# One-core attention and feed-forward block: causal mask for the row maxima added by VectorE instead of TensorE, layer norm spread over GpSimd and ScalarE, and a separate step order for each engine

## The reference

```python
xn = layernorm(x)                                    # over the last axis, eps 1e-5
q, k, v = xn @ Wq.T, xn @ Wk.T, xn @ Wv.T            # 16 heads of 16
att = q @ k.T / sqrt(16) + causal_mask               # per batch and head, 512 x 512
s = (softmax(att) @ v) @ Wo.T
gate, up = silu(qlinear(xn, wq_gate)), qlinear(xn, wq_up)   # 256 -> 704, integer weights less 128, times scale
g = silu(qlinear(gate * up, wq_down))                # 704 -> 256
out = x + s * g
```

## Time and profile before

| what | value |
|---|---|
| median of 3 runs | 343.9 us (339.8 to 346.67) |
| the profiled execution | 341.76 us |
| its span, first to last instruction | 340.0 us |
| mean granted TensorE clock | 0.975 |

### The profile page before, as it was taken

How to read it: one execution, slowest core, us unless ns; L and a number is a source line. 1 busy time by engine, 2 the same in 40 slices (tenths; PEclk the granted TensorE clock), 3 DMA queues, 4 the chain that set the end, 5 groups by cost and what they waited for, 6 DMA issues and landing times.

```text
span 340.0 us, 6041 instructions
## 1 busy us (share of the span) xinstructions
PE 304.1 (89%) x2352; PEld 207.2 (61%) x2352; DVE 215.4 (63%) x359; ACT 168.1 (49%) x239; POOL 133.2 (39%) x190
## 2 busy tenths in 40 slices
PE   0688688999999989999999999999999999998873
PEld 0566456787565547688665556688665656884433
DVE  5799787445569986646568986646465656455223
ACT  3527134634556655524456655524466666235830
POOL 4077344411254563202354463202355563123351
PEclk9999697999999999999999999999999999999996
DMA  7947671049670004078580010078590020010201
GB/s 281 255 155 174 188 119 63 4 155 151 191 128 1 2 3 126 13 201 155 178 143 2 2 64 2 7 191 144 188 157 4 0 67 4 0 35 31 66 0 64
DMA packets 21008, 31.56 MB, mean 93 GB/s; under 512 B 2148, under 2 KB 9956, under 8 KB 20980
## 3 DMA queue, kind: packets, MB, share of 16 engines
q1 hardware_dynamic: 20528, 30.50, 37.2%
q10 hardware_dynamic: 452, 0.67, 0.5%
HBM read 20.32 MB, written 10.49 MB: 91 GB/s over the span
## 4 chain that ended last, share of the span: by engine, by line
PE 70%; DVE 21%; ACT 3%; issue 2%; DMA 2%; POOL 0%; ACTq 0%; SPq 0%; DVEq 0%
PE ps L349 15%; PE ps L351 12%; PE ps L350 12%; PE ps L519 10%; PE ps L500 7%; PE ps L459 6%; PE ps L471 4%; DVE mx L958 2%; DVE mx L960 2%; DVE hid L945 2%; DVE nw L919 2%; DVE xn L926 2%; PE ps L527 2%; ACT hid L654 2%; DVE nw L920 1%
## 5 line engine op out<-in xcount | busy, mean ns | idle before, releaser
L859 POOL TENSOR_SCALAR_AFFINE_SELECT pt<-pt 128x256 f32<-128x256 f32 (+1 forms) x112 | 48.1, 443 | 117.3 <-ACT pt L719 117.3
L719 ACT ACTIVATE pt<-ps 128x1024 f32<-128x1024 f32 x80 | 81.8, 1023 | 23.6 <-PE ps L500 23.5
L827 POOL TENSOR_TENSOR hl<-hid,hh 128x512 fp32r<-128x512 f32 x24 | 31.2, 1300 | 42.7 <-ACT hh L668 42.3
L958 DVE TENSOR_REDUCE mx<-ps 128x2 f32<-128x1024 f32 x32 | 39.0, 1221 | 12.8 <-PE ps L471 12.4
L459 PE MATMUL ps<-kp,qp 48*128 48x512 f32 (+3 forms) x256 | 37.2, 350 | 10.9 <-DVE mx L958 6.9
L519 PE MATMUL ps<-pt,vt 128*17 128x256 f32 (+3 forms) x512 | 43.8, 437 | 1.2 <-POOL pt L859 1.1
L349 PE MATMUL ps<-xh,guh 128*128 128x512 f32 x96 | 43.2, 450 | 1.5 <-DVE u L939 1.5
L500 PE MATMUL ps<-qp,kp 50*128 50x512 f32 (+3 forms) x256 | 40.4, 373 | 2.5 <-DMA qp<-ctr 2.2
L821 POOL TENSOR_TENSOR hid<-hid 128x512 f32<-128x512 f32 x24 | 32.2, 1342 | 21.5 <-ACT hid L661 21.3
L351 PE MATMUL ps<-xh,gul 128*128 128x512 f32 x96 | 38.5, 401 | 0.0
L350 PE MATMUL ps<-xl,guh 128*128 128x512 f32 x96 | 38.3, 399 | 0.0
(11 more groups left out here) (107 smaller groups left out, 538.9 us busy)
## 6 DMA issues: line engine op xcount, KB each, us to landing
qk_scratch<-hid SPq DMA_DIRECT2D x24, 256.0 KB
qp<-qk_scratch SPq DMA_DIRECT2D x14, 256.0 KB, 4.7
kp<-qk_scratch SPq DMA_DIRECT2D x14, 256.0 KB, 6.8
qp<-qk_scratch SPq DMA_DIRECT2D x18, 128.0 KB, 5.1
kp<-qk_scratch SPq DMA_DIRECT2D x18, 128.0 KB, 7.2
xr<-in_x SPq DMA_DIRECT2D x4, 512.0 KB, 3.8
out<-xr SPq DMA_DIRECT2D x8, 256.0 KB, 2.2
xin<-in_x SPq DMA_DIRECT2D x3, 512.0 KB, 3.9
```

Source lines behind the costliest of these rows:

```text
L719: nc.scalar.activation(pt[:, 2 * kk:2 * kk + 2, :], ps[:, base:base + 2, :], ACT.Exp, scale=SCALE).then_inc(exp_done, 1)
L859: mm = nc.gpsimd.affine_select(out=diag, in_=diag, compare_op=ALU.is_ge, fill=0.0, base=0, pattern=[[0, diag.shape[1]], [1, P]], channel_m ...
L958: mm = nc.vector.tensor_reduce(mg[:, :, kk, 3], both, AX.X, ALU.max, negate=True)
```

## The change

- From the ninth pair on (`n >= LEAD`), TensorE's 4 mask matmuls of a pair are left out. VectorE adds a float32 triangle `tri` (128 x 128, broadcast) to the diagonal blocks in PSUM, in place, and waits for its own addition (`tri_added`) before it reduces. Pairs 0 to 7 of batch 0 keep the matmuls.
- The inverse root for batches 1 to 3 goes to GpSimd (`root`): 2 operations, three times 4, and 2 more that make `shf` = -mean * root, 16 in all, each waiting for the one in front. The first guess is made in one operation instead of two.
- The normalisation of batches 1 to 3 goes to ScalarE (`Identity` with scale and bias). VectorE keeps the statistics and their aggregation (`moments`).
- `hsg` and `sgt` are made by GpSimd.
- `FILL` is replaced by four tables, one for each engine, with 20 steps each. TensorE does the units first, then the scores, then the maxima.
- SP stores all four chunks of q and k first, then `c_rows(b, 2)`, then the first half of `stack`; the second half comes after `c_rows(b, 3)`.

```diff
+TENSOR_STEPS = (
+    [("pv", -1, 10), ("pv", -1, 11), ("s", 0, 0), ("m", 0, 8)],
+    [("zt", -1, 3), ("v", 0, 0), ("s", 0, 1), ("m", 0, 9)],
+    [("v", 0, 1), ("s", 0, 2), ("m", 0, 10)],
+    [("t", 1, 0), ("t", 1, 1), ("z2", -1, 1), ("pv", 0, 0), ("s", 0, 3), ("m", 0, 11)],
+    [("c", 0, 1), ("qk", 1, 0), ("qk", 1, 1), ("s", 0, 4), ("m", 0, 12)],
+    [("dn", 0, 0), ("s", 0, 5), ("m", 0, 13)],
+    [("qk", 1, 2), ("pv", 0, 1), ("s", 0, 6), ("m", 0, 14)],
+    [("dn", 0, 1), ("s", 0, 7), ("m", 0, 15)],
+    [("qk", 1, 3), ("o", -1, 0), ("pv", 0, 2), ("s", 0, 8), ("m", 0, 16)],
+    [("gu", 1, 0), ("c", 0, 2), ("pv", 0, 3), ("s", 0, 9), ("m", 0, 17)],
+    [("zt", 0, 0), ("gu", 1, 1), ("pv", 0, 4), ("s", 0, 10), ("m", 0, 18)],
+    [("o", -1, 1), ("gu", 1, 2), ("pv", 0, 5), ("s", 0, 11), ("m", 0, 19)],
+    [("gu", 1, 3), ("gu", 1, 4), ("s", 0, 12), ("m", 1, 0)],
+    [("gu", 1, 5), ("zt", 0, 1), ("s", 0, 13), ("m", 1, 1)],
+    [("c", 0, 3), ("gu", 1, 6), ("s", 0, 14), ("m", 1, 2)],
+    [("pv", 0, 6), ("gu", 1, 7), ("s", 0, 15), ("m", 1, 3)],
+    [("z2", 0, 0), ("gu", 1, 8), ("s", 0, 16), ("m", 1, 4)],
+    [("gu", 1, 9), ("pv", 0, 7), ("s", 0, 17), ("m", 1, 5)],
+    [("pv", 0, 8), ("c", 1, 0), ("gu", 1, 10), ("s", 0, 18), ("m", 1, 6)],
+    [("zt", 0, 2), ("gu", 1, 11), ("s", 0, 19), ("m", 1, 7), ("pv", 0, 9)],
+)
...
+VECTOR_STEPS = (
+    [],
+    [("max", 0, 8)],
...
+    [("max", 1, 1), ("norm", 0, 1)],
+    [("max", 1, 2), ("gate", 1, 3)],
+    [("max", 1, 3), ("zlo", 0, 0)],
+    [("max", 1, 4), ("gate", 1, 4)],
+    [("max", 1, 5)],
+    [("max", 1, 6), ("gate", 1, 5), ("norm", 0, 2), ("max", 1, 7)],
+)
...
@@ tensor: maxima
-                for r in range(2):
+                for r in range(2 if n < LEAD else 0):
...
@@ vector: maxima
+                if STEPS * b + m >= LEAD:
+                    if kk < 2:
+                        diag = both[:, :, 3 * P:]
+                        mask = tri[:].rearrange("p (o n) -> p o n", o=1).to_broadcast([P, 2, P])
+                    else:
+                        diag = (both[:, :, 2 * P:].rearrange("p e (a n) -> p e a n", a=2) if kk < 4 else
+                                both.rearrange("p e (a c n) -> p e a c n", a=2, c=2)[:, :, :, 1, :])
+                        mask = tri[:].rearrange("p (o q n) -> p o q n", o=1, q=1).to_broadcast([P, 2, 2, P])
+                    if STEPS * b + m == LEAD:
+                        dve.wait_ge(consts, 3)
+                    nc.vector.tensor_tensor(diag, diag, mask, ALU.add).then_inc(tri_added, 1)
+                    dve.wait_ge(tri_added, STEPS * b + m - LEAD + 1)
...
@@ gpsimd
+            def root(b, n):
+                v, y, t = nw[:, 0, :], nw[:, 1, :], nw[:, 2, :]
+                if n == 0:
+                    pool.wait_ge(mv_done, TT * b)
+                    pool.wait_ge(xn_done, TT * b)
+                    root_op(nc.gpsimd.tensor_scalar(v, mv[:, :, 1], EPS, None, ALU.add))
+                    root_op(nc.gpsimd.tensor_scalar(y.bitcast(I32), v.bitcast(I32), -0.5, MAGIC, ALU.mult, ALU.add))
+                    return
+                root_op(nc.gpsimd.tensor_tensor(t, y, y, ALU.mult))
+                root_op(nc.gpsimd.tensor_tensor(t, t, v, ALU.mult))
+                root_op(nc.gpsimd.tensor_scalar(t, t, -0.5, 1.5, ALU.mult, ALU.add))
+                root_op(nc.gpsimd.tensor_tensor(y, y, t, ALU.mult))
+                if n == NEWTON:
+                    root_op(nc.gpsimd.tensor_tensor(t, mv[:, :, 0], y, ALU.mult))
+                    nc.gpsimd.tensor_scalar(shf[:], t, -1.0, None, ALU.mult).then_inc(shf_done, 1)
...
@@ scalar
+            def normalise(b, i):
+                if i == 0:
+                    act_e.wait_ge(shf_done, b)
+                    act_e.wait_ge(xt_ready, KD * b)
+                nc.scalar.activation(xn[:, i, :], xin[:, i, :], ACT.Identity, scale=nw[:, 1, i:i + 1],
+                                     bias=shf[:, i:i + 1]).then_inc(xn_done, 1)
...
@@ sync
                 if b + 1 < B:
-                    store_qk(b + 1, 0)
-                    store_qk(b + 1, 1)
+                    for c in range(4):
+                        store_qk(b + 1, c)
+                c_rows(b, 2)
+                if b + 1 < B:
                     stack(b + 1, 0, 0)
                     stack(b + 1, 0, 1)
-                    store_qk(b + 1, 2)
-                    store_qk(b + 1, 3)
-                c_rows(b, 2)
                 if b:
                     store_out(b - 1, 0)
                     store_out(b - 1, 1)
+                c_rows(b, 3)
                 if b + 1 < B:
                     stack(b + 1, 1, 0)
                     stack(b + 1, 1, 1)
-                c_rows(b, 3)
```

More of the change, by code:

```diff
@@ new lines @@
+GPSIMD_STEPS = (
+    [("hlo", 0, 4), ("hid", 0, 5)],
+    [],
+    [("hlo", 0, 5), ("mask", 0, 0)],
+    [("mask", 0, 1)],
+    [("mask", 0, 2)],
+    [("mask", 0, 3)],
+    [("mask", 0, 4)],
+    [("mask", 0, 5)],
+    [("mask", 0, 6)],
+    [("mask", 0, 7)],
+    [("mask", 0, 8)],
+    [("res", -1, 0), ("hid", 1, 0), ("mask", 0, 9)],
+    [("hlo", 1, 0), ("mask", 0, 10)],
+    [("root", 2, 0), ("res", -1, 1), ("hid", 1, 1), ("mask", 0, 11)],
+    [("root", 2, 1), ("hlo", 1, 1), ("hid", 1, 2), ("mask", 0, 12)],
+    [("root", 2, 2), ("mask", 0, 13)],
+    [("root", 2, 3), ("hlo", 1, 2), ("mask", 0, 14), ("hid", 1, 3)],
+    [("mask", 0, 15)],
+    [("hlo", 1, 3), ("hid", 1, 4), ("mask", 0, 16)],
+    [("mask", 0, 17), ("mask", 0, 18), ("mask", 0, 19)],
+)
@@ L72, with entries @@
 HEAD_MIX = HEAD[6:]
[L75 to L84, removed]
+HEAD_DONE = {(k, 0, n) for k in ("t", "qk", "gu", "xhi", "xlo", "qhi", "qlo", "tanh", "up", "hhi", "gate", "hid", "hlo")
+             for n in range(2 * HT)}
+HEAD_DONE |= {("c", 0, 0), ("ccp", 0, 0)} | {(k, b, i) for k in ("bn", "mom", "root", "xn") for b in range(2) for i in range(TT)}
+def entries(engine, steps, b, s):
+    first = FIRST[engine].get(s, []) if b == 0 else []
+    last = LAST[engine].get(s, []) if b == B - 1 else []
+    todo = [(kind, b + o, n) for kind, o, n in steps[s] if 0 <= b + o < B]
+    return [x for x in todo if x not in HEAD_DONE] + [(kind, b + o, n) for kind, o, n in first + last]
 def tail_units():
@@ L92 @@
 OWN_BANK = {("z2", B - 1, 1): ST, ("o", B - 1, 0): MX, ("o", B - 1, 1): MX + 1}
-IN_RING = [u for u in HEAD + [u for b in range(B) for s in range(STEPS) for u in step_units(b, s)] + tail_units()
-           if u[0] not in ("pv", "m", "r") and u not in OWN_BANK]
+IN_RING = [u for u in HEAD + [u for b in range(B) for s in range(STEPS) for u in entries("tensor", TENSOR_STEPS, b, s)]
+           + tail_units() if u[0] not in ("pv", "m", "s", "r") and u not in OWN_BANK]
 BANK = {u: RING + n % 3 for n, u in enumerate(IN_RING)}
@@ L571, in unit @@
                     project_out_part(b, n, 0, bank).then_inc(oa_ready, 1)
+                elif kind == "s":
+                    scores(b, n)
                 elif kind == "m":
@@ L601, in _ @@
                 for s in range(STEPS):
-                    scores(b, s)
-                    if STEPS * b + s + LEAD < STEPS * B:
-                        maxima(*divmod(STEPS * b + s + LEAD, STEPS))
-                    for kind, of, n in step_units(b, s):
+                    for kind, of, n in entries("tensor", TENSOR_STEPS, b, s):
                         unit(kind, of, n)
@@ L871, in unit, with root_op @@
                     residual_first(b, n)
+            root_at = [0]
+            def root_op(ins):
+                ins.then_inc(root_step, 1)
+                root_at[0] += 1
+                pool.wait_ge(root_step, root_at[0])
+            def root(b, n):
[13 more added lines that the diff above has]
+                    nc.gpsimd.tensor_scalar(shf[:], t, -1.0, None, ALU.mult).then_inc(shf_done, 1)
             for kind, b, n in HEAD_MIX:
                 unit(kind, b, n)
+                if kind == "gu" and n in (5, 7):
+                    for k in range(2):
+                        root(1, n - 5 + k)
+            work = {"root": root, "mask": mask, "hid": hidden, "hlo": hidden_lo, "res": residual, "oa": residual_first}
             for b in range(B):
                 for s in range(STEPS):
-                    mask(b, s)
-                    if s == last_hidden_step(b):
-                        hidden_lo(b, HT - 1)
-                    for kind, of, n in step_units(b, s):
-                        unit(kind, of, n)
+                    for kind, of, n in entries("gpsimd", GPSIMD_STEPS, b, s):
+                        work[kind](of, n)
             for kind, of, n in tail_units():
@@ L1102, in _ @@
                 if (kind, n) == ("gu", 0):
[L1103 to L1106 removed]
+                    moments(1, 0)
                 if (kind, n) == ("gu", 3):
```

116 lines of the change are left out of this document (77 added, 39 removed), and 20 rows, old and new, of the table FILL.

## The result

| | before | changed |
|---|---|---|
| median (4 runs each) | 342.98 us (339.8 to 346.67) | 322.74 us (320.13 to 325.29) |
| profiled execution, its span | 341.76, 340.0 us | 323.56, 321.5 us |
| mean granted TensorE clock | 0.975 | 0.971 |

The changed kernel takes 0.9414 of the time before, with a 95% interval of 0.9292 to 0.9535: faster by 5.9%. Timed again on another chip (experiment 5) it took 0.9525 (0.9468 to 0.9581). Some executions run over 1.5% longer than the fastest of the same kernel, mostly at a lower granted clock; the ratios leave these out, and since the profiled executions of experiments 3 and 10 are such, no lengths are read in them.

A forecast was written before the change was run, and what follows sets the result against it. TensorE was taken as the bound. From 341.8 us, -20.3 (mask), -3 (layer norm), -1.5 (head) and +3.5 (order) gave 320.5, scaled to the median as 322.5 and rounded to 322 us; range 313 to 337.

The forecast's parts named there:

- The mask on TensorE: In TensorE's queue, pairs 8 to 79 lose mask blocks priced at 0.22 or 0.32 us each: 20.3 us saved.
- The additions: On VectorE, 72 mask additions of 0.42 or 0.69 us, 42.1 us in all, fitting beside other work: nothing added.
- the third rival: GpSimd holds VectorE's additions by +1.1 us each, making the kernel slower, near 355 us; chance 0.03.
- Layer norm off VectorE: In the steps, removing Newton's operations and the normalisation from VectorE's queue takes 3 us off 11.7 us of waits.
- the head's 1.5: In the head, VectorE's delay before the awaited reduction shrinks: 1.5 us saved, between 0 and 4.
- The order: New tables and SP's queue make shifts, units and reload meet later: +3.5 us, bounds -4 and +12.
- the first rival: The order is better than allowed, removing the steps' waits and 4 us in the head: below 315 us; chance 0.10.
- Reload behind the shift: On SP's queue, the first half of `stack` behind `c_rows(b, 2)`, some 11 us ahead of use: part of 1.5 us.
- The last shift: In the last batch, the fourth group's shift moves from step 12 to 14, so TensorE waits about 2 us.
- The second rival: VectorE becomes the pace where its gates and projections meet the additions: 330 to 341 us; chance 0.20.
- the 0.75 us that VectorE's 8.6 were worth: Batch 2, with 8.6 us less on VectorE, lasts 0.75 us less than batch 1; so VectorE isn't the bound.
- if windows shrink by less than the mask blocks: Sign of being wrong: batch windows shrinking by less than the mask blocks would mean VectorE is the pace.

The follow-up runs named there:

- experiment 5: The changed kernel unaltered, timed again in another job beside three edited kernels: 325.67 us, ratio 0.9525 to the kernel before.
- experiment 3: The changed kernel with Newton's steps and the normalisation of batches 1 to 3 back on VectorE: 328.32 us, ratio 0.9554 to the kernel before.
- experiment 10: The kernel before with only the four step tables and SP's order changed, mask on TensorE, layer norm on VectorE: 331.98 us, ratio 0.9694.
- experiment 9: The kernel before with only layer norm and the gate's factors moved to GpSimd and ScalarE; old order, mask on TensorE: 334.93 us, ratio 0.9786.
- experiment 1: The changed kernel with the mask of all pairs back on TensorE; new order and moved layer norm kept: 330.0 us, ratio 0.9637 to the kernel before.
- experiment 12: The changed kernel with no mask on the maxima from the ninth pair on, leaving out part of the computation: 318.26 us, ratio 0.9334 to the kernel before.
- L: Part of the change: layer norm and the small factors on GpSimd and ScalarE; alone on the kernel before, ratio 0.9786.
- O: Part of the change: the order, that is four step tables and SP's queue; alone on the kernel before, ratio 0.9694.
- M: Part of the change: the mask added by VectorE from the ninth pair on; alone on the kernel before, ratio 1.0455.
- experiment 4: The changed kernel with every addition on VectorE made twice: 343.78 us, ratio 1.0028 to the kernel before.
- experiment 11: The kernel before with the mask on VectorE and layer norm moved, in the old order: 339.99 us, ratio 0.9918.
- experiment 7: The changed kernel with SP issuing the first half of the reload ahead of the last two stores and the third shift: 321.04 us, ratio 0.9394 to the kernel before.
- experiment 2: The kernel before with only the mask addition moved to VectorE; old order, layer norm and SP's queue: 358.33 us, ratio 1.0455.
- experiment 8: The changed kernel with the earlier reload, the last batch's fourth shift two steps earlier and the head's first shift earlier: 318.93 us, ratio 0.9344 to the kernel before.

## Why the prediction was right, and where its terms were not

The total came out: 322 us forecast, 322.7 measured. Its terms did not. That it came within 1 us is luck: the mask's price was 8.2 us too high and the additions' 5.6 too low, and of the order, forecast as a loss, a gain of 5.2 came. What holds of the mechanism is that taking work from TensorE's queue pays and that VectorE takes the additions at their free duration. Going from before over experiments 9, 1 and 12, one part at a time, the spans give each term:

| step | spans | measured | forecast |
|---|---|---|---|
| L, the head with it | 340.0 to 333.2 | -6.8 | -3 and -1.5 |
| O | 333.2 to 328.0 | -5.2 | +3.5 |
| M, mask blocks off TensorE | 328.0 to 315.9 | -12.1 | -20.3 |
| M, additions on VectorE | 315.9 to 321.5 | +5.6 | 0 |
| sum | 340.0 to 321.5 | -18.5 | -21.3 |

Each span is that of one execution, and the spans of the changed kernel alone range from 318.0 to 325.6 us, so a row is good to some 3 us. By the ratios the four rows are -7.3, -5.1, -10.4 and +2.7 us (+6.5 with experiment 5). Another path gives other numbers, because the parts are not independent. The ratios of all eight combinations:

| | old order | new order |
|---|---|---|
| neither M nor L | 1 | 0.969 |
| L | 0.979 | 0.964 |
| M | 1.046 | 0.955 |
| M and L | 0.992 | 0.941, again 0.953 |

**The mask on TensorE: mis-sized.** "A block of 4 mask matmuls costs the distance to the next instruction" was the step that failed. 20.3 us was the price of 72 distances; experiments 1 and 12 have 12.1, the spacing with and without a block 13.3. The distance from a block's start to the next unit contains a gap that any last instruction ahead of that unit has.

**The additions: durations right, their price wrong.** 42.1 us were forecast, 42.8 measured, at 0.43 and 0.70 us. None of the 72 was held: they range over 0.415 to 0.700 us, while GpSimd was busy 143 us. So the third rival falls. (By its own figures, 1.06 less 0.16, it should also have had +0.9 us an addition and not +1.1, which makes its 78 to 87 us some 74 to 83.) The Trainium skill, "SBUF — State Buffer", section "Who interferes with whom", says the same of an instruction with a single SBUF input outside the 2-port modes; the trace agrees. But I had them at nothing beside other work. They cost 5.6 us, 4.7 of them in the last batch, where I had counted waits "about what that batch has now". Experiment 4 is the stronger test: the next 42.8 us cost 20.8. A sum that fits a window doesn't say that each cycle fits its step.

**Layer norm off VectorE: sign right, too small.** With the head it is 6.8 us against 4.5. I took 3 of the 11.7 us of waits in the steps; in batch 1 alone 4.0 of 4.7 went (experiment 9). For the head's 1.5, 1.85 came (first scores at 50.05 us in experiment 9), at one wait: the maxima that start at 37.32 us in the earlier trace rows start at 35.22 in experiment 9 and, behind 2.11 us of waiting instead of 4.26, at 35.20 in the changed kernel:

```profile
35.20 0.50 PE L542 MATMUL ps<-kp,qp 48*128 48x384 f32 x4 [2.11 <-DVE mx L1101]
```

A cost that I had not seen: the normalisation itself was held by GpSimd. Its line in the kernel before (ns min/median/max):

```profile
L926 DVE TENSOR_SCALAR xn<-xin,mv,nw x16: 399/908/1475, 8.5 to 204.6; 128x256 f32<-128x256 f32 x16
```

All eight instances in steps 16 to 19, and one of the head's, end just behind one of GpSimd's two-input products (0.91 to 1.48 us); the seven with no product beside them take 0.40 to 0.41. One ran from 194.94 to 196.33 us, GpSimd's L827 beside it from 194.89 to 196.18. One view of one line would have told it; I had read only Newton's. On ScalarE none of the 12 was held (0.589 to 0.608 us). The page cited above (the Trainium skill, "SBUF — State Buffer", section "Who interferes with whom") names `tensor_scalar` among the operations that can enter a 2-port mode and then meet GpSimd's lock; the trace agrees, with 0.40 us free and 1.39 held.

ScalarE's normalisation takes 0.60 us and not 0.37, and no engine's wait is put down to it. A Newton operation on GpSimd takes 0.20 us busy and 0.28 to the next, well under the 1.27 of my upper end. The Trainium skill, "Perfetto Trace Analysis", section "Optimizing Scalar/DVE Operations", had it that a move from VectorE to GpSimd might not help. Experiment 9 decides against it here, at 2.1%, for GpSimd's and ScalarE's share of the move together.

**The order: wrong sign.** I forecast +3.5 us, as I priced only what the new tables make late. By itself the order gains 3.1% (experiment 10), and with M in it 9 points (1.046 to 0.955): the first rival ("the order is better than I allow") in part. What it does with M is shown by the waits of weight loads on reductions, with M and L in both: 17.1 us in the old order (experiment 11), 5.4 in the new one. What it does without M or waits is less clear. From experiment 9 to experiment 1 the head is 0.8 us shorter, batch 0 is 2.5 us longer (1.6 of them a wait for the reload), and batches 1, 2 and 3 are 2.4, 1.6 and 2.9 shorter. In batch 1 (73.6 to 71.3) the waits of weight loads on other engines fall from 2.0 to 0.7 us, and the idle time put down to "issue" ahead of them from 15.7 to 14.4. So half is waits that the order removes; that units in another order also leave smaller gaps is argued, not shown.

**Reload behind the shift: the mechanism right, the size too small.** I allowed it a part of 1.5 us. The waits in the batches sum to 3.2, and experiment 7 gains 1.4%. The "some 11 us" ahead of its use are there: in batch 0 the third shift is issued at 85.18 us and the reloaded keys are wanted at 95.67. But I set nothing against them. The reload's issues take until 90.28, and its last part, issued at 89.85, lands 7.5 us later, at 97.4.

**The last shift: shown.** Forecast: a wait of about 2 us on `ctr`'s DMA in the last batch and none elsewhere. The changed kernel there:

```profile
296.00 0.30 PE L562 MATMUL ps<-ident,cn 128*128 128x128 f32 x1
...
299.85 0.80 PE L585 MATMUL ps<-qp,kp 50*128 50x512 f32 x2 [2.14 <-DMA qp<-ctr]
300.57 1.11 PE L620 MATMUL ps<-ident,zbuf 128*128 128x128 f32 x4
301.62 0.79 PE L585 MATMUL ps<-qp,kp 50*128 50x512 f32 x2
```

2.14 us stand in the matmuls' row, 3.06 in the weight load's. Again the score pairs behind it take 0.79 us, with a granted clock of 0.5 (the 0.50 in this window, columns as in the earlier trace rows):

```profile
302.00:305.80 3.80, 3.80 (x30) 1.14 (x28) 0.69 (x1) 2.12 (x3) 0.59 (x2) 0.50 0.00 0
```

In experiment 7, with the same wait, they don't:

```profile
298.34 0.49 PE L586 MATMUL ps<-qp,kp 50*128 50x512 f32 x2 [2.12 <-DMA qp<-ctr]
...
299.35 0.50 PE L586 MATMUL ps<-qp,kp 50*128 50x512 f32 x2
```

That batch lasts 46.1 us (46 was forecast) against 48.7, at a granted clock of 1.00 against 0.93 (and 50.1 at 0.87 in experiment 5). Of the 4.7 us that the additions cost in the last batch, some 2.6 thus go with the clock of that execution, and 2.1 (46.1 less 44.0) with the loop.

**The second rival**, VectorE as the pace, is false in the changed kernel (additions nearly free in batches 0 to 2) and true in the old order (experiment 2) and with the doubled addition (experiment 4). What speaks against it, "the 0.75 us that VectorE's 8.6 were worth", was read from a window that ends 2 us late (it is 2.8 us), and it compares two batches with different units; experiment 9 takes the same work away in the same batch and has 3.5 us.

**Signs forecast and found:** L471's matmuls down to 32 (now L556, 32); windows near 69, 71, 71 and 46, found 71.8, 69.1, 68.3 and 48.8; VectorE at 56 to 60 us in batch 1, found 53.6, below the range (its base of 44.5 came from that late window; cut at 277.4 it is 43.3); waits of the maxima on VectorE under 12 us, found 5.4. "None elsewhere" for `ctr` missed the head, where the first shift is waited for, 2.89 us in the matmuls' row at 49.74; the kernel before had 1.75 there. One sign of being wrong did appear: "if windows shrink by less than the mask blocks". By the forecast's prices the blocks are 5.6 us in a full batch and 3.4 in the last; batch 0 shrank by 2.4 and the last one by nothing. In batch 0 the cause isn't the one I had named: the additions cost 0.2 us there, while the order makes it longer (above).

**Open:** what sets the clock behind a wait, and with it why the same kernel reads 0.9414 in one job and 0.9525 in another (their mean clocks are 0.971 and 0.952); why the order without M gains in batches 1 to 3 and loses in batch 0; how O's gain divides between the four tables and TensorE's doing the units first, and L's between GpSimd and ScalarE, which no run separates; and whether experiment 8 is faster than 7.

## What to carry to other kernels

The price of a small instruction on the bounding engine is the spacing of its neighbours with it less that without it; read the second from a place in the same trace where the two neighbours meet without it, not from the distance to the next start. When work goes onto an engine that sits in a short loop, ask for each step how much lies ahead of the looped operation in its queue; the batch's sum doesn't tell it. Cut windows at the same kind of instruction in every batch before comparing their lengths: a cut 2 us off turned a difference of 2.8 us into 0.75. And an edit's worth depends on its surroundings (here from +4.6% to about -2%), so a part that loses when tried alone may pay once the order is made for it.

## What was not expected of the hardware

A stop of TensorE of some 2 us can be followed by half its granted clock: the score pairs took 0.79 us instead of 0.50 behind a wait of 1.93 us (experiment 2) and of 2.14 us (the changed kernel, last batch). It doesn't always: behind a wait of 2.12 us they took 0.50 (experiment 7). So the same program gives different times for the same wait. In experiment 2 TensorE is busy for 304.3 us, against 304.1 before, though 288 matmuls are gone. An estimate from the mean clocks fits: (1 - 0.934) x 356.1 = 23.5 us of full clock missing, against (1 - 0.975) x 340.0 = 8.5 before, so 15 us more, near the 16.2 of busy time that the changed kernel saves.

The hold of VectorE by GpSimd, isn't limited to tiny operations: the normalisation of 128 x 256 elements, with one tensor from SBUF, took 0.40 us free and up to 1.48 beside a two-input product of GpSimd, while additions with PSUM as one input kept to 0.700 us at most.
